# Self-attention heads computed in pairs on small array tiles, and weight rounding in eight pieces

## The chip, the core and the metric

The kernel is one launch on one core of a Trainium2 chip. The core's engines are TensorE (PE), VectorE (DVE), ScalarE (ACT), GpSimd (POOL) and SyncE (SP, which issues the DMAs). The metric is the device time of a launch in microseconds (us).

## The reference

One block of a Perceiver-like model over 256 tokens of width 512: cross-attention to 4096 context rows (16 heads), then self-attention (16 heads of 32 channels), then a feed-forward layer whose weights are rounded to -1, 0 or 1. All of it in float32. The change lies in the second and third parts:

```python
# x: (1, 256, 512)
x = x + _L0_xattn_ref(_layernorm(x), ctx_512, ...)          # cross-attention, untouched
# self-attention, H = 16 heads, Dh = 32
qkv = einsum('bsd,df->bsf', Xn, W_in);  Q, K, V = split(qkv, 3)
Q, K = _rope(Q), _rope(K)
scores = einsum('bhqd,bhkd->bhqk', Q, K) / sqrt(Dh)
probs = softmax(scores, axis=-1)
ctx = einsum('bhqk,bhkd->bhqd', probs, V)
x = X + einsum('bsd,df->bsf', ctx, W_out)
# feed-forward; weight_quant for w1, w2, w3:
scale = 1.0 / clip(mean(abs(w)), EPS)
wq = clip(round(w * scale), -1.0, 1.0) / scale
h = silu(bitlinear(x, w1)) * bitlinear(x, w3);  x = x + bitlinear(h, w2)
```

## The kernel before

The program is written engine by engine. Each engine runs its instructions in the order in which they are written, and semaphores (`wait_ge`, `then_inc`) order them across engines. There are two token tiles t of 128 tokens, and the 16 heads lie in four groups g of four heads a, so that a group fills 128 channels.

Up to about 495 us runs the cross-attention, which the diff doesn't touch. Then come two layer norms, and for each token tile three projections (K, Q, V; `project`, L764). V of tile 1 is done in two halves, the second after the first scores. Queries and keys are copied to SBUF (`natural_copy`), rotated on VectorE (`rotate`, four small instructions with two SBUF inputs, L1356 to L1362), transposed on TensorE, and copied again.

Keys go to `kbd`, a block-diagonal tile: 128 rows (channels of a group) by 16 heads by 256 keys, zero outside the 32 rows of each head (`k_rows`, L367, two copies on VectorE and two on ScalarE for each tile). Values go to `vbd` in the same way (`value_copies`, L1372, four small copies a tile). GpSimd writes the zeros ahead (L533, L535). With the zeros, one full 128-row product gives the scores of one head, for all of its 128 queries.

The attention loop goes by groups. A unit u is a group g and a token tile t, so there are eight units. On TensorE `head_scores(u)` (L802) makes two products of 512 columns. VectorE's `maxima(u)` takes the negated maxima of four heads from PSUM (L1415) and multiplies these 128x4 numbers by the score scale (L1416); ScalarE's `exponentials(u)` (L1091) makes four exponentials with that bias and scale and their sums; `normalise(u)` on VectorE takes a reciprocal (L1406) and multiplies the four heads' probabilities in SBUF (L1408). TensorE transposes the probabilities head by head (`head_transposes`, L814), VectorE and ScalarE copy them out in turns (`probabilities_out`, L1422 and L1099), and `head_product` (L828) multiplies them with `vbd`; the four heads of a group add into one PSUM tile, which VectorE copies out to `cT` (L1454). Two units' scores lie in PSUM at a time (banks 4 to 7). The output projection (L856, L860) and the feed-forward layer follow.

Beside the loop the weights of the feed-forward layer are prepared. ScalarE sums the absolute values in quarters (`abs_sum`, L1047), TensorE and VectorE make a scale of them (`weight_sum`, `weight_total`, `weight_scale`), GpSimd multiplies and rounds each weight in two passes over 128x5632 elements (`weight_magic`, L543, and `weight_round`, L548), and VectorE clips the result (`clip`, L1426). GpSimd's first rounding pass waits for the last projection; each of the magic passes waits for its scale.

Of the kernel before, what the change touches and what calls it, by code (L numbers as in the profile page):

```python
# [5 lines left out]
TOK = 256  # L6
TT = TOK // 128
# [20 lines left out]
def program(nc, x_in, ctxT, kcos, ksin, qcos, qsin, wq, wkcq, wqr, wkr, wkv, wo,  # L28
# [16 lines left out]
    ASCALE = float(DH) ** -0.5  # L45
    ctx = ExitStack()
    with ctx:
# [55 lines left out]
        prob = at("prob", C, [128, 4, HPG, TOK])  # L103
# [66 lines left out]
        anb = small("anb", [128, 8, HPG])  # L170
# [27 lines left out]
        anb_done = sem("anb_done")  # L198
# [5 lines left out]
        bd_zero = sem("bd_zero")  # L204
# [99 lines left out]
        kbd_done = [sem(f"kbd_done{k}") for k in range(2)]  # L304
# [58 lines left out]

        def k_rows(copy, t, a):

            part = slice(a * DH, (a + 1) * DH)
            return copy(kbd[part, a::HPG, t * 128:(t + 1) * 128], bank(t)[part, :].rearrange("p (g k) -> p g k", g=FG))  # L367
# [103 lines left out]
        def _(pool):  # L471
# [60 lines left out]
            pool.wait_ge(av_done, 16 * XH)  # L532
            nc.gpsimd.memset(vbd[:, :, :, :], 0.0).then_inc(bd_zero, 1)  # L533
            pool.wait_ge(xo_done, TT)
            nc.gpsimd.memset(kbd[:, :, :], 0.0).then_inc(bd_zero, 1)  # L535
# [5 lines left out]
            def weight_magic(j, wf):  # L541
                pool.wait_ge(wscale_done, j + 1)
                nc.gpsimd.tensor_scalar(wf[:, :], wf[:, :], wscale[:, j:j + 1], MAGIC, ALU.mult, ALU.add)\  # L543
                    .then_inc(wmagic_done, 1)

            def weight_round(j, wf, wb):
                pool.wait_ge(wmagic_done, j + 1)
                nc.gpsimd.tensor_scalar(wb[:, :], wf[:, :], -MAGIC, 1.0, ALU.add, ALU.mult).then_inc(wround_done, 1)  # L548
# [5 lines left out]
            pool.wait_ge(wround_done, 1)  # L554
# [11 lines left out]
        def _(pe):  # L566
# [213 lines left out]
            for t in range(TT):  # L780
# [5 lines left out]
                if t == 0:  # L786
                    pe.wait_ge(v_copied, HPG)
                    project(1, 2, range(DK // 2))
            def head_scores(u):

                g, t = u // 2, u % 2
                if u == 0:
                    pe.wait_ge(qkn_done, 2 * TT)
                if u == 1:
                    pe.wait_ge(wmean_done, 1)
                if u < 2:
                    pe.wait_ge(qT_done, t + 1)
                wait(pe, aexp_done, 4 * (u - 1))
                for a in range(2):
                    if u == 0:  # L800
                        pe.wait_ge(kbd_done[a], 2 * TT)
                    last = nc.tensor.matmul(bank(4 + u % 2 * 2 + a), qT[:, t, g, :],  # L802
                                            kbd[:, 4 * g + 2 * a:4 * g + 2 * a + 2, :].rearrange("p h k -> p (h k)"),
                                            start=True, stop=True)
                last.then_inc(ascore_done, 1)

            def head_transposes(g, a):

                pe.wait_ge(prob_done, 4 * (2 * g + 1) + a + 1)
                wait(pe, pT_done[a % 2], 2 * g + a // 2)  # L810
                for k in range(TT):
                    for t in range(TT):
                        o = (k * TT + t) * 128
                        last = nc.tensor.transpose(bank(a % 2, o, o + 128),  # L814
                                                   prob[:, (2 * g + t) % 4, a, k * 128:(k + 1) * 128], ident[:, :])
                last.then_inc(apT_done, 1)

            def head_product(g, a):

                if a == 0:  # L820
                    wait(pe, cT_done, g - 1)
                    if g == 1:
                        pe.wait_ge(v_copied, 2 * HPG)
# [756 lines left out]
```

## Time and profile before

| | us |
|---|---|
| median of 3 runs | 617.68 (617.29 to 619.96) |
| the profiled execution, its own time | 613.68 |
| span of its trace | 611.8 |
| mean granted TensorE clock | 0.974 of full |
| TensorE busy, whole span | 549.7 |
| VectorE busy, whole span | 513.5 |
| ScalarE busy, whole span | 369.3 |
| GpSimd busy, whole span | 161.6 |

The span is the time from the first to the last instruction; the launch's own time is 1.9 us longer. Of this execution the stretch from about 512 us to 577 us is the self-attention, and all of the diff lies in it. A row of the trace gives the start, the duration, the engine, the line of the kernel, the operation and the tiles; "x4" means four records in a row, and the bracket at the end names who ended the idle time ahead of it. A float32 product shows as two records.

### The profile page before, as it was taken

Reading aid. Unit: us, or ns where it says so; the run is one execution under the profiler, and the core shown is the slowest. Engines: PE = TensorE matmul, PEld = TensorE weight load, DVE = VectorE, ACT = ScalarE, POOL = GpSimd, SP = SyncE. Lnnn points to the kernel's source line nnn. Section 1 sums busy time; section 2 is a strip of 40 time slices with the busy share of each in tenths; the row PEclk is TensorE's granted clock in tenths of the full one; section 3 lists DMA queues with packets and bytes.
Section 4 is the critical chain, followed back from the end, with each engine's and each line's share of the span. In section 5 each row is a group of like instructions: output and inputs, shape, how many; then the busy total and the mean of one; then the engine's idle time right before and its main releaser. Section 6 shows DMA issues by size and latency. Waiting matters only on the chain.

```text
span 611.8 us, 9932 instructions
## 1 busy us (share of the span) xinstructions
PE 549.7 (90%) x3762; PEld 380.0 (62%) x3762; DVE 513.5 (84%) x782; ACT 369.3 (60%) x435; POOL 161.6 (26%) x148
## 2 busy tenths in 40 slices
PE   6788986838999999999999999999979998688996
PEld 3677774415666666666766676676668854355543
DVE  5478988785989999999999999999968555898786
ACT  3312321583878687877878787878785338654332
POOL 2446678300220221021012202220101243455001
PEclk9799998988999999999999999999999999989999
DMA  9983311799999999999999999999999875000000
GB/s 315 349 245 126 116 54 50 129 361 201 201 195 199 196 196 201 201 210 210 210 209 202 204 197 204 197 203 205 196 193 166 347 276 219 1 0 1 2 0 34
DMA packets 290412, 107.38 MB, mean 176 GB/s; under 512 B 282704, under 2 KB 283728, under 8 KB 288080
## 3 DMA queue, kind: packets, MB, share of 16 engines
q1 hardware_dynamic: 290384, 107.01, 80.5%
q8 instruction: 17, 0.28, 0.2%
q14 instruction: 11, 0.09, 0.0%
HBM read 37.26 MB, written 0.52 MB: 62 GB/s over the span
## 4 chain that ended last, share of the span: by engine, by line
PE 63%; DVE 18%; DMA 6%; issue 5%; ACT 4%; SPq 2%; POOL 1%; DVEq 0%; ACTq 0%; POOLq 0%
PE ps L656 15%; PE ps L658 8%; PE ps L638 8%; PE ps L640 8%; PE ps L639 8%; DMA pT<-split 5%; PE ps L764 3%; PE ps L828 2%; DVE rows L1272 2%; DVE split L1254 2%; DVE qrope L1298 2%; DVE qrot L1304 1%; PE ps L802 1%; DMA keys<-ctxT 1%; PE ps L606 1%
## 5 line engine op out<-in xcount | busy, mean ns | idle before, releaser
L656 PE MATMUL ps<-pT,VH 128*128 128x256 f16 x1024 | 196.2, 273 | 9.3 <-DMA pT<-split 9.2
L658 PE MATMUL ps<-pT,VL 128*128 128x128 f16 x1024 | 182.9, 219 | 0.0
L1272 DVE TENSOR_SCALAR_CACHE_REDUCE rows<-ps,qback 128x1024 f32<-128x1024 f32 x128 | 163.5, 1279 | 23.0 <-PE ps L640 23.0
L1016 ACT ACTIVATE split<-rows,rz 128x2048 f16<-128x2048 f32 x64 | 124.7, 1994 | 75.9 <-DVE rz L1218 73.6
L1254 DVE SCALAR_TENSOR_TENSOR split<-rows,rz,split 128x2048 f16<-128x2048 f32 x64 | 150.2, 2348 | 1.3 <-issue 1.2
L656 PEld LDWEIGHTS ps<-pT,VH 128*128 128x128 f16 x1024 | 100.4, 98 | 49.4 <-issue 10.8
L1002 ACT ACTIVATE rows<-rows,negm 128x2048 f32<-128x2048 f32 x64 | 127.2, 1988 | 2.9 <-DVE negm L1277 2.9
L658 PEld LDWEIGHTS ps<-pT,VL 128*128 128x128 f16 x1024 | 100.5, 98 | 27.6 <-issue 0.3
L521 POOL TENSOR_TENSOR ctx_c<-acc 128x128 f32<-128x128 f32 x32 | 26.0, 814 | 303.1 <-ACT acc L991 303.1
L638 PE MATMUL ps<-KH,qcur 128*128 128x512 f16 x256 | 97.8, 382 | 8.4 <-DVE rows L1272 5.0
L640 PE MATMUL ps<-KH,qcur 128*128 128x512 f16 x256 | 97.8, 382 | 0.0
L639 PE MATMUL ps<-KL,qcur 128*128 128x512 f16 x256 | 97.8, 382 | 0.0
L487 POOL TENSOR_TENSOR qrope<-qrope,qrot 128x768 f32<-128x768 f32 x16 | 35.3, 2205 | 43.2 <-DVE qrot L1304 43.2
L640 PEld LDWEIGHTS ps<-KH,qcur 128*128 128x128 f16 x256 | 25.2, 98 | 30.7 <-issue 0.8
L962 ACT ACTIVATE KH<-keys,kscale 128x512 f16<-128x512 f32 x8 | 5.8, 722 | 55.7 <-DVE keys L1310 46.7
L638 PEld LDWEIGHTS ps<-KH,qcur 128*128 128x128 f16 x256 | 25.2, 99 | 15.3 <-DVE rows L1272 6.7
L719 PE MATMUL ps<-qrope,wqr_sb 128*128 128x256 f32 x96 | 24.5, 392 | 7.0 <-ACT qrT L967 4.0
L639 PEld LDWEIGHTS ps<-KL,qcur 128*128 128x128 f16 x256 | 25.2, 98 | 2.4 <-issue 0.3
L691 PE MATMUL ps<-hT_hi,wq_hi 128*128 128x256 f32 x64 | 20.3, 317 | 6.6 <-ACT qhk L945 5.1
L719 PEld LDWEIGHTS ps<-qrope,wqr_sb 128*128 128x128 f32 x96 | 18.1, 194 | 12.3 <-POOL qrope L487 5.7
L828 PE MATMUL ps<-pT,vbd 128*128 128x256 f32 x64 | 19.2, 438 | 7.0 <-DVE pT L1422 7.0
L703 PE MATMUL ps<-qhk,wkcq_sb 128*128 128x256 f32 x96 | 23.6, 384 | 1.3 <-DVE qrot L1304 1.3
(188 smaller groups left out, 802.2 us busy)
## 6 DMA issues: line engine op xcount, KB each, us to landing
w_sb<-w SPq DMA_DIRECT2D x3, 2816.0 KB, 15.1
wq_sb<-wq SPq DMA_DIRECT2D x4, 1024.0 KB, 8.5
wo_sb<-wo SPq DMA_DIRECT2D x4, 1024.0 KB, 10.8
wkcq_sb<-wkcq SPq DMA_DIRECT2D x4, 768.0 KB, 5.9
keys<-ctxT SPq DMA_DIRECT2D x2, 1024.0 KB, 8.4
stage<-ctxT SPq DMA_DIRECT2D x16, 128.0 KB, 3.2
stage<-kcos SPq DMA_DIRECT2D x8, 256.0 KB, 3.3
stage<-ksin SPq DMA_DIRECT2D x8, 256.0 KB, 3.5
```

What stands on the lines that cost most here:

```text
L487: nc.gpsimd.tensor_tensor(qrope[:, h % 2], qrope[:, h % 2], qrot[:, h % 2], ALU.add).then_inc(qrope_done, 1)
L638: nc.tensor.matmul(o, q[0], KH[:, key], start=True, stop=False)
L639: nc.tensor.matmul(o, q[0], KL[:, key], start=False, stop=False)
L640: last = nc.tensor.matmul(o, q[1], KH[:, key], start=False, stop=True)
L656: nc.tensor.matmul(bank(6 + r % 2, 0, 256), VH[:, 4 * b + k, :], p.rearrange("p x q -> p (x q)"), start=(b == 0 and k == 0), stop=False)
L658: last = nc.tensor.matmul(bank(6 + r % 2, 0, 128), VL[:, 4 * b + k, :], p[:, 0, :], start=False, stop=(b == 7 and k == 3))
L719: last = nc.tensor.matmul(bank(6, 0, TOK), wqr_sb[:, h % 2, h // 2 * QC + c, :], qrope[:, h % 2, c * TOK:(c + 1) * TOK], start=(h % 2 == 0 ...
L828: last = nc.tensor.matmul(bank(2 + g % 2, 0, TOK), vbd[:, k, 4 * g + a, :], pT[:, a, k, :], start=(a == 0 and k == 0), stop=(a == HPG - 1 ...
L1002: nc.scalar.activation(part, part, ACT.Exp, bias=negm[:, k:k + 1], accum_out=zpart[:, k, half:half + 1]).then_inc(exp_done, 1)
L1016: nc.scalar.activation(split[:, split_slot(r, half), :, 0, :], rows[:, k, half * 2048:(half + 1) * 2048].rearrange("p (b k) -> p b k", k=1 ...
L1254: nc.vector.scalar_tensor_tensor(out=split[:, split_slot(r, half), :, 1, :], in0=rows[:, k, half * 2048:(half + 1) * 2048].rearrange("p (b ...
L1272: nc.vector.tensor_scalar(rows[:, k, c * 1024:(c + 1) * 1024], ps[:, score_bank(s) * 512:(score_bank(s) + 2) * 512], qback[:, r // 2:r // ...
```

## The change

- The block-diagonal tiles and the GpSimd passes that zero them are gone. `kT` holds the keys plainly, 128 rows by 4 groups by 256 keys, and `v_sb` the values; each is filled by one copy for each tile.
- A unit v is now a pair of heads of one group, with both token tiles; there are again eight (`UNITS`). The scores of a head come from its 32 rows alone (`tile_position` with a row offset), four products of 256 columns a unit. The products with the values write 32 columns of the array (a column offset), four of 256 columns a unit, and no longer add over the heads.
- The score scale is put into the copy of the queries (`scale=ASCALE` in the copy to `qT`). The 128x4 multiplication of the maxima is gone.
- GpSimd's six weight passes are written as eight pieces of 128x704 each.
- The loop is written in another order on the three engines.

```diff
+    WPIECES = 8
+    UNITS = AH // 2
-        kbd = at("kbd", D + 16 * KB, [128, AH, TOK])
-        vbd = at("vbd", C + 16 * KB, [128, TT, AH, 128])
+        kT = at("kT", D + 16 * KB, [128, FG, TOK])
+        v_sb = at("v_sb", C + 16 * KB, [128, TT, DM])
...
             def weight_magic(j, wf):
                 pool.wait_ge(wscale_done, j + 1)
-                nc.gpsimd.tensor_scalar(wf[:, :], wf[:, :], wscale[:, j:j + 1], MAGIC, ALU.mult, ALU.add)\
-                    .then_inc(wmagic_done, 1)
+                for k in range(WPIECES):
+                    part = slice(k * DK * FF // WPIECES, (k + 1) * DK * FF // WPIECES)
+                    nc.gpsimd.tensor_scalar(wf[:, part], wf[:, part], wscale[:, j:j + 1], MAGIC, ALU.mult, ALU.add)\
+                        .then_inc(wmagic_done, 1)
...
+            def head_scores(v):
+
+                g, first = v // 2, v % 2 * 2
...
+                for t in range(TT):
+                    for x in range(2):
+                        part = slice((first + x) * DH, (first + x + 1) * DH)
+                        last = nc.tensor.matmul(bank(4 + v % 2 * 2 + x, t * TOK, (t + 1) * TOK), qT[part, t, g, :],
+                                                kT[part, g, :], start=True, stop=True, tile_position=((first + x) * DH, 0))
                 last.then_inc(ascore_done, 1)
...
+                for k in range(TT):
+                    for x in range(2):
+                        a = first + x
+                        o = (2 + g % 2) * 512
+                        last = nc.tensor.matmul(ps[a * DH:(a + 1) * DH, o:o + TOK],
+                                                v_sb[:, k, (4 * g + a) * DH:(4 * g + a + 1) * DH], pT[:, a, k, :],
+                                                start=(k == 0), stop=(k == TT - 1), tile_position=(0, a * DH))
...
+            head_scores(0)
+            head_scores(1)
+            for v in range(UNITS):
+                head_transposes(v)
+                if v + 2 < UNITS:
+                    head_scores(v + 2)
...
+                if v >= 1:
+                    head_products(v - 1)
+            head_products(UNITS - 1)
...
+            exponentials(0)
+            for v in range(UNITS):
+                if v + 1 < UNITS:
+                    exponentials(v + 1)
+                probabilities_out(v)
+                if v < 4:
+                    abs_sum(2, v)
...
+            value_copies(1)
+            maxima(0)
+            maxima(1)
+            weight_total(1)
+            for v in range(UNITS):
+                normalise(v)
+                if v + 2 < UNITS:
+                    maxima(v + 2)
...
+                probabilities_out(v)
+                if v == 5:
                     clip(0, w1b)
```

TensorE before, from the last two products of group 0 through the scores and transposes of the units 4 and 5 (`prob` is the probabilities, `pT` their transposes):

```order
L828 MATMUL ps<-pT,vbd 128x256 [waits pT_done1]
L828 MATMUL ps<-pT,vbd 128x256
L802 MATMUL ps<-kbd,qT 128x512 [waits aexp_done]
L802 MATMUL ps<-kbd,qT 128x512
L814 MATMUL ps<-ident,prob 128x128 [waits pT_done0,prob_done]
L814 MATMUL ps<-ident,prob 128x128 x3
L814 MATMUL ps<-ident,prob 128x128 [waits pT_done1,prob_done]
L814 MATMUL ps<-ident,prob 128x128 x3
L802 MATMUL ps<-kbd,qT 128x512 [waits aexp_done]
L802 MATMUL ps<-kbd,qT 128x512
```

TensorE after, one whole unit in the same part of the program:

```order
L813 MATMUL ps<-ident,prob 128x128 [waits pT_done0,prob_done]
L813 MATMUL ps<-ident,prob 128x128 x3
L813 MATMUL ps<-ident,prob 128x128 [waits pT_done1]
L813 MATMUL ps<-ident,prob 128x128 x3
L801 MATMUL ps<-kT,qT 128x256 [waits aexp_done]
L801 MATMUL ps<-kT,qT 128x256 x3
L832 MATMUL ps<-pT,v_sb 32x256 [waits pT_done1,pT_done0]
L832 MATMUL ps<-pT,v_sb 32x256 x3
```

Before, the scores of the group ahead stand in front of the transposes of this one. Now the transposes of a unit stand in front of the scores of the unit two ahead, and the products of the unit behind close the round.

VectorE before, one group of the loop:

```order
L1415 TENSOR_REDUCE anm<-ps 128x4 [waits ascore_done]
L1416 TENSOR_SCALAR anb<-anm 128x4 [waits dve_chain]
L1422 COPY pT<-ps 128x512 [waits apT_done]
L1415 TENSOR_REDUCE anm<-ps 128x4 [waits ascore_done]
L1416 TENSOR_SCALAR anb<-anm 128x4 [waits dve_chain]
L1422 COPY pT<-ps 128x512 [waits apT_done]
L1406 RECIPROCAL arz<-az 128x4 [waits aexp_done]
L1408 TENSOR_SCALAR prob<-prob,arz 128x256 [waits dve_chain]
L1408 TENSOR_SCALAR prob<-prob,arz 128x256 x3
L1406 RECIPROCAL arz<-az 128x4 [waits aexp_done]
L1408 TENSOR_SCALAR prob<-prob,arz 128x256 [waits dve_chain]
L1408 TENSOR_SCALAR prob<-prob,arz 128x256 x3
```

VectorE after, one unit of the loop and the start of the next:

```order
L1391 RECIPROCAL arz<-az 128x4 [waits aexp_done]
L1394 TENSOR_SCALAR prob<-prob,arz 128x256 [waits dve_chain]
L1394 TENSOR_SCALAR prob<-prob,arz 128x256 x3
L1400 TENSOR_REDUCE anm<-ps 128x4 [waits ascore_done]
L1406 COPY pT<-ps 128x512 [waits aav_done,apT_done]
L1391 RECIPROCAL arz<-az 128x4 [waits aexp_done]
L1394 TENSOR_SCALAR prob<-prob,arz 128x256 [waits dve_chain]
```

The L1416 rows are gone. The maxima of a unit now stand right behind the normalisation of the unit two behind it, and ahead of the copy of that unit's transposes.

## Rows read from the trace of the kernel before

**Rows 1.** Busy time by stretch: PE, PEld, DVE, ACT, POOL; clock; DMA.

```profile
533.00:545.00 12.00, 8.97 (x30) 6.35 (x31) 11.86 (x14) 3.51 (x14) 9.84 (x2) 0.73 0.00 0
545.00:557.00 12.00, 12.00 (x54) 8.21 (x53) 9.36 (x30) 9.31 (x28) 0.00 (x0) 1.00 0.01 1
```

**Rows 2.** Chain that ended last, in time: start, us, engine, tile, line.

```profile
514.79 3.23 DVE rot_tmp L1356
...
527.47 4.86 DVE prob L1408 x4
...
535.02 3.92 DVE anb L1416
...
574.85 1.82 PE ps L828 x8
```

**Rows 3.** One line of VectorE over 500 to 612 us: busy, mean ns, idle before.

```profile
L1416 DVE TENSOR_SCALAR anb<-anm 128x4 f32<-128x4 f32 x8 | 14.6, 1822 | 0.3
```

**Rows 4.** Timeline of DVE: a rotation, the loop, and the first clip.

```profile
511.13 0.42 DVE L1356 TENSOR_TENSOR rot_tmp<-qkn,acs 128x256 f32<-128x256 f32 x1 [1.40 <-ACT qkn L1053]
...
546.47 0.18 DVE L1406 RECIPROCAL arz<-az 128x4 f32<-128x4 f32 x1 [0.64 <-ACT prob L1091]
546.68 1.14 DVE L1408 TENSOR_SCALAR prob<-prob,arz 128x256 f32<-128x256 f32 x4
...
548.46 1.22 DVE L1415 TENSOR_REDUCE anm<-ps 128x4 f32<-128x1024 f32 x1 [0.31 <-PE ps L802]
...
549.80 0.69 DVE L1422 COPY pT<-ps 128x512 f32<-128x512 f32 x1
...
571.78 1.61 DVE L1426 TENSOR_SCALAR w1b<-w1b 128x5632 bf16<-128x5632 bf16 x1
```

**Rows 5.** Timeline of POOL in the self-attention: start, us, engine, line, operation.

```profile
533.96 4.96 POOL L543 TENSOR_SCALAR w_sb<-w_sb,wscale 128x5632 f32<-128x5632 f32 x1 [2.55 <-DVE wscale L1384]
```

**Rows 6.** Timeline of PE in the loop.

```profile
532.87 1.97 PE L814 MATMUL ps<-ident,prob 128*128 128x128 f32 x8 [4.30 <-DVE prob L1408]
...
546.54 1.88 PE L802 MATMUL ps<-kbd,qT 128*128 128x512 f32 x4
548.26 1.04 PE L814 MATMUL ps<-ident,prob 128*128 128x128 f32 x8
549.13 1.88 PE L802 MATMUL ps<-kbd,qT 128*128 128x512 f32 x4
```

**Rows 7.** Timeline of ACT, first and fifth exponential of the loop.

```profile
524.50 0.47 ACT L1091 ACTIVATE prob<-ps,anb 128x256 f32<-128x256 f32 x1 [1.40 <-DVE anb L1416]
...
526.31 0.48 ACT L1091 ACTIVATE prob<-ps,anb 128x256 f32<-128x256 f32 x1
```

**Rows 8.** Timeline of DVE in the first stage, where POOL works beside it.

```profile
35.98 0.69 DVE L1310 TENSOR_TENSOR keys<-keys,stage 128x512 f32<-128x512 f32 x1
36.59 1.81 DVE L1223 TENSOR_TENSOR ksum<-kpart 128x1 f32<-128x1 f32 x1
```

**Rows 9.** Timeline of POOL in the same stage.

```profile
36.03 2.35 POOL L487 TENSOR_TENSOR qrope<-qrope,qrot 128x768 f32<-128x768 f32 x1 [5.62 <-DVE qrot L1304]
38.35 1.27 POOL L500 TENSOR_TENSOR keys<-keys,stage 128x512 f32<-128x512 f32 x1
...
71.03 2.31 POOL L487 TENSOR_TENSOR qrope<-qrope,qrot 128x768 f32<-128x768 f32 x1 [3.85 <-DVE qrot L1304]
73.31 1.71 POOL L500 TENSOR_TENSOR keys<-keys,stage 128x512 f32<-128x512 f32 x1
```

**Rows 10.** Timeline of DVE again, a product of keys between two POOL instructions.

```profile
72.46 1.43 DVE L1314 SCALAR_TENSOR_TENSOR KL<-keys,kscale,KH 128x512 f16<-128x512 f32 x1 [0.79 <-ACT KH L962]
```

**Rows 11.** Busy time by half microsecond, columns as in Rows 1.

```profile
518.00:518.50 0.50, 0.00 (x0) 0.00 (x0) 0.47 (x4) 0.50 (x1) 0.00 (x0) 1.00 0.00 0
...
533.00:533.50 0.50, 0.50 (x3) 0.50 (x4) 0.50 (x3) 0.00 (x0) 0.00 (x0) 0.50 0.00 0
...
536.50:537.00 0.50, 0.50 (x2) 0.00 (x0) 0.50 (x1) 0.00 (x0) 0.50 (x1) 1.00 0.00 0
```

More of the change, by code:

```diff
@@ L303, in program @@
         zsum_done = sem("zsum_done")
-        kbd_done = [sem(f"kbd_done{k}") for k in range(2)]
+        kT_done = sem("kT_done")
         ctx_in = [sem(f"ctx_in{k}") for k in range(2)]
@@ L795, in head_scores @@
                     pe.wait_ge(wmean_done, 1)
[L796 to L804, printed above, removed]
@@ L805, in head_scores @@
-                last.then_inc(ascore_done, 1)
[L807 to L816, printed above, removed]
@@ new lines, in head_scores, with head_transposes @@
+                last.then_inc(ascore_done, 1)
+            def head_transposes(v):
+                pe.wait_ge(prob_done, 4 * (v + 1))
+                for x in range(2):
+                    wait(pe, pT_done[x], v)
+                    for k in range(TT):
+                        for t in range(TT):
+                            o = (k * TT + t) * 128
+                            last = nc.tensor.transpose(bank(x, o, o + 128), prob[:, v % 4, x, t, k * 128:(k + 1) * 128],
+                                                       ident[:, :])
+                    last.then_inc(apT_done, 1)
@@ L821, in head_product, with head_products @@
+            def head_products(v):
+                g, first = v // 2, v % 2 * 2
+                if first == 0:
                     wait(pe, cT_done, g - 1)
-                    if g == 1:
-                        pe.wait_ge(v_copied, 2 * HPG)
+                    if g == 0:
+                        pe.wait_ge(v_copied, 2)
                     if g % 2 == 0:
                         pe.wait_ge(wmean_done, g // 2 + 2)
-                pe.wait_ge(pT_done[a % 2], 2 * g + a // 2 + 1)
+                for x in range(2):
+                    pe.wait_ge(pT_done[x], v + 1)
@@ L1084, in _ @@
             abs_sum(1, 3)
-            def exponentials(u, first=0, end=HPG):
-                act.wait_ge(anb_done, u + 1)
-                if u >= 4:
-                    act.wait_ge(apT_done, 4 * (u // 2 - 1))
-                for a in range(first, end):
-                    nc.scalar.activation(prob[:, u % 4, a, :], bank(4 + u % 2 * 2 + a // 2, a % 2 * TOK, (a % 2 + 1) * TOK),
-                                         ACT.Exp, bias=anb[:, u, a:a + 1], scale=ASCALE,
-                                         accum_out=az[:, u, a:a + 1]).then_inc(aexp_done, 1)
@@ L1418, in probabilities_out, with normalise @@
-            def probabilities_out(g, a):
-                dve.wait_ge(apT_done, 4 * g + a + 1)
-                wait(dve, aav_done, 4 * (g - 1) + a + 1)
-                nc.vector.tensor_copy(pT[:, a].rearrange("p k t -> p (k t)"), bank(0)).then_inc(pT_done[0], 1)
+            def normalise(v):
+                dve.wait_ge(aexp_done, 4 * (v + 1))
+                link(nc.vector.reciprocal(arz[:, v, :], az[:, v, :]))
+                for k in range(4):
+                    part = prob[:, v % 4, k // 2, k % 2, :]
+                    nc.vector.tensor_scalar(part, part, arz[:, v, k:k + 1], None, ALU.mult).then_inc(prob_done, 1)
@@ new lines, in maxima, with probabilities_out @@
+            def maxima(v):
+                dve.wait_ge(ascore_done, v + 1)
+                b = 4 + v % 2 * 2
+                src = ps[:, b * 512:(b + 2) * 512].rearrange("p (a k) -> p a k", a=4)
+                nc.vector.tensor_reduce(anm[:, v, :], src, AX.X, ALU.max, negate=True).then_inc(anm_done, 1)
+            def probabilities_out(v):
+                dve.wait_ge(apT_done, 2 * v + 1)
+                wait(dve, aav_done, v - 1)
+                nc.vector.tensor_copy(pT[:, v % 2 * 2].rearrange("p k t -> p (k t)"), bank(0)).then_inc(pT_done[0], 1)
@@ L1455, in _ @@
+            context_copy(FG - 1)
+            clip(1, w3b)
             clip(2, w2b)
```

159 lines of the change are left out of this document (48 added, 111 removed).

## Prediction, made before the changed kernel was run

> **What bounds the kernel now.** I read four views. First the table by stretch [rows 1]: between 545 and 557 us, where GpSimd rests, TensorE is busy for 12.00 of 12.00 us at full clock; in the stretch before, where GpSimd works for 9.84 us, TensorE falls to 8.97 of 12, its clock to 0.73, and VectorE is busy for 11.86. Second the chain of waits in time [rows 2]: the last product of the loop ends at 574.85 + 1.82 = 576.67 us, and the chain runs through three kinds of long VectorE rows, a rotation of 3.23 us, four normalisations of 4.86 us together, a 128x4 multiplication of 3.92 us. Third the line of those 128x4 multiplications [rows 3]: eight of them take 14.6 us. Fourth the timelines: four normalisations alone take 1.14 us [rows 4], and the 3.92 us one of the chain begins at 535.02 and ends at 538.94, as GpSimd's pass ends (533.96 + 4.96 = 538.92, [rows 5]). So VectorE instructions of this kind, from SBUF to SBUF, stand still until GpSimd's instruction is over. Reductions and copies out of PSUM do not.
>
> The stalls add up to about 20 us: 14.6 less eight times 0.17 gives 13.2, the normalisations 4.86 less 1.14 give 3.7, and the rotation 3.23 less the 0.42 us of its like [rows 4] gives 2.8. What is left is bound by TensorE.
>
> The Trainium skill, "SBUF — State Buffer", section "SBUF: two separate sides", says that VectorE and GpSimd share a pair of ports as an exclusive lock, held for a whole instruction, with the loser fully blocked. The stalls above agree. The page does not say who comes next when both wait.
>
> **What goes and what takes its place, with GpSimd and the clock left out.** The new loop is one chain per unit. On VectorE a unit's normalisation stands ahead of the maxima of the unit two ahead; TensorE has transposes ahead of the scores that these maxima wait for. Nothing of this overlaps. The terms:
> - normalisation 0.21 + 1.14 = 1.35 [rows 4], and 0.05 to reach TensorE;
> - transposes of two heads 549.13 - 548.26 = 0.87 [rows 6];
> - scores. Before, two products of 512 columns take 548.26 - 546.54 = 1.72 [rows 6]. Four of 256 columns are as many columns. No row shows array tiles: if both row tiles run side by side it is half, 0.86; if not, 1.72 and whatever a change of tile shape costs. Below 0.86 nothing can go, since two tiles are used. Each float32 product is two records, and records of one head must follow each other, so only the second of one head and the first of the next overlap; I take 1.3;
> - 0.20 from TensorE to VectorE (548.26 to 548.46), maxima 1.22, copy of the transposes 0.60 of its 0.69 [rows 4, 6].
>
> Together 5.6 us a unit (5.15 to 6.0). Before, a unit where GpSimd rests costs 1.72 + 0.87 + 1.82 = 4.4, TensorE's own work [rows 2, 6]. So the pairs relieve TensorE, which then idles, and put a latency chain in its place.
>
> The start: the rotation begins at 514.8, takes 1.2 alone (the 0.42 of its first instruction [rows 4], and 0.8 for the three behind it), and about 0.3 + 3 x 0.65 more by GpSimd's pieces (below); with 0.44 of transposes and 1.73 of the second half of V it puts the first scores at 520.4, against 521.05. The copies to kT (2 in place of 4) and v_sb are hidden behind that half of V; were they not, they would cost 0.7. Then 1.3 + 0.2 + 1.22 and four exponentials at (526.31 - 524.50)/4 = 0.45 each with 0.2 to hand over [rows 7]: the first normalisation at 525.2. Six units of 5.6 reach 558.8. VectorE also has in this chain one clip of 1.6 [rows 4], two copies to cT of 0.34 and two weight scales of 0.33, together 3.0: 561.8. The last two units lack scores and maxima: 2.6 to the last normalisation, then 1.35 + 0.9 + 0.2 + 0.6 + 0.1 and a product of 1.3 (0.87 to 1.82): **568.9**, 7.8 less than 576.67. The ScalarE work in a unit (1.8 of exponentials, 0.5 of copy, 1.5 of sums in the first four) is under 5.6 and hidden; if the unit were shorter than 3.9 it would bind. The removed zeroing passes ran while GpSimd had nothing else due: nothing. The clips of w3 and w2, now 3.2 us behind the last cT copy, lie beside 4.3 us of output projection: nothing, a slack of 1.1.
>
> **GpSimd in pieces.** A piece is 4.96/8 = 0.62 us [rows 5]; I allow 0.05 between pieces. Forty of the 48 lie in the loop. What counts is who goes next when both engines want the pair. The first stage shows both sides [rows 8, 9]. At 35.98 VectorE multiplies keys, GpSimd's L487 starts at 36.03 and waits; VectorE's next, L1223, one element wide, stands directly behind (36.59) and still takes 1.81 us, to 38.40, as L487 ends at 38.38. So a waiting GpSimd goes ahead of a queued VectorE instruction. In the other direction, L500 at 73.31, queued right behind L487, takes 1.71 us against 1.27 at 38.35 [rows 9], since VectorE's L1314, waiting since 72.46 [rows 10], goes first. The two take turns. A long pass made VectorE wait once; now the four multiplications of a unit each wait for a piece: 0.3 for the first and 0.65 for the other three, 2.25 a unit. Forty pieces with VectorE's turns between them take 27 + 5 = 32 us of a loop of some 45, so about five of eight units: 5 x 2.25 + 0.3 for the clip = **11.5**. Bounds: 1.8 (one wait of 0.3 for each) and 18 (all eight). This gives 580.4, 3.7 later than before.
>
> **The clock.** Before, TensorE idled for 4.30 us to 532.87 [rows 6]; at 533.0 the granted clock is 0.50, its lower level of 1.2 GHz, and at 536.5 again 1.00, after TensorE had worked through [rows 11]. Eight transposes took 1.97 there in place of 1.04. A shorter pause at 518 left it at 1.00 [rows 11]. In a unit with pieces TensorE now idles from the end of a product to the next transposes: 0.2 + 1.22 + 0.6 + 1.35 + 2.25 - 1.3 = 4.3 us, the length that made it fall. Transposes and scores, 2.2 us of the chain, then double, for as long as the stretch above (533.0 to under 536.5, some 3.5 us) lasted: 1.75 lost each time. I take three in the five units: **5.3** (0 to 8.8); units without pieces idle for 2.0 and cost nothing. Sum: 568.9 + 11.5 + 5.3 = 585.7, **9.0 later**. Everything behind the loop (the output projection and the feed-forward) keeps its order and length. The profiled execution took 613.68, so 622.7 by it; the median of the runs is 4.0 higher, and on that I forecast 617.68 + 9.0 = 626.7.
>
> **Rivals.**
> - *Turns, but the clock holds*: 3.7 later, 621.4. For: small matrices keep TensorE working more often than in one block. Against: the idle time of 4.3. Chance 0.20.
> - *VectorE keeps the pair over its four multiplications*, since they come back to back and overlap. Then 1.8 stands for 11.5, idle times shrink, two falls of the clock at most: 568.9 + 1.8 + 3.5 = 574.2, 2.5 earlier, 615.2, and 611.7 with no fall. It decides from the point where a unit waits less than about 0.5 us, one piece. Against: L1223, which also stood back to back. Chance 0.18, two thirds of it faster.
> - *The array tiles don't overlap, and each change of shape costs*: scores at 1.72 and 0.2 (as long as TensorE takes to hand a result over, the nearest row) at two changes in a unit's chain: 0.82 x 6 + 1 = 6 more, 632.7. Chance 0.14.
> - The forecast: 0.48.
>
> The Trainium skill has two rules on this. "TensorE: Matmul & The Clock Gate", "Part 3: Packing small matmuls — row/col tiling", has several tiles take one product's time and some 4 ns for each tile more; by it the scores are 0.87, and the end 3 us earlier, 623.7. "TensorEngine Tiling (Array Packing)", "Key Properties", speaks against the change: a change of tiling mode drains TensorE, and there are three in each unit; that is the third rival. No row here shows either.
>
> **How the numbers follow.** About 0.5% (3.1 us) is what this kernel's measurement tells from no change: 614.6 to 620.8. Faster: two thirds of the second rival, 0.12. Same: the rest of it and half of the first, 0.16. Slower: 0.72. The range goes from 614 (second rival with one fall) to 634 (third rival with a little more): about one in ten on each side.
>
> **What would show it.** Right: L1394's total is far over 32 x 0.28 = 9 us, with many rows near 0.9 us in the stretches where GpSimd works, while reductions stay at 1.2; the granted clock is 0.50 in several stretches of the loop; normalisation to normalisation takes 5.6 in a quiet unit. Wrong: L1394 rows wait once a unit (second rival), four score products take 0.86 or over 1.9 us at full clock, or GpSimd's pieces take well over 0.67 with nobody waiting. The end of the loop, 576.67 before, is the one number to compare.

## The result, and the profile after

The changed kernel takes 626.52 us (median of 4 runs, 624.9 to 628.32) against 617.48 for the kernel before: ratio 1.0139, 95% interval 1.0094 to 1.0183. That is slower, by 9.0 us or 1.4%, clear of the noise but a small change. The profiled execution took 625.16, its span is 623.4. The loop that the diff rewrites runs from the first scores to the first product of the output projection, from 520.89 to 587.98 us: 67.1 us, against 55.5 before (521.05 to 576.51). What follows it takes as long as before (623.4 - 588.0 = 35.4, before 611.8 - 576.5 = 35.3). So the loss lies in the loop.

Busy time by stretch of the changed kernel (us, PE, PEld, DVE, ACT, POOL, granted clock, DMA), as in [rows 1] and [rows 11]:

```profile
522.00:523.50 1.50, 0.04 (x4) 0.00 (x0) 1.43 (x2) 0.92 (x3) 1.50 (x3) 1.00 0.00 0
...
525.00:526.50 1.50, 0.00 (x0) 0.00 (x0) 1.17 (x3) 1.50 (x9) 1.50 (x3) 0.50 0.00 0
...
553.50:555.00 1.50, 1.50 (x9) 1.17 (x9) 0.00 (x0) 0.10 (x1) 0.00 (x0) 0.50 0.00 0
...
583.50:585.00 1.50, 1.50 (x8) 0.76 (x5) 0.10 (x1) 0.00 (x0) 0.00 (x0) 0.50 0.00 0
...
586.50:588.00 1.50, 1.50 (x17) 0.60 (x12) 0.00 (x0) 1.48 (x2) 0.00 (x0) 1.00 0.00 0
```

TensorE pauses from about 522.0 us, its clock falls during this first pause (at about 524.7 us), and it stays at 0.50, the lower level of 1.2 GHz, until about 586.1 us, 2 us before the end of the loop. TensorE's rows show both the chain and the clock; the bracket is the pause ahead of the row:

```profile
520.89 1.16 PE L801 MATMUL ps<-kT,qT 32*128 32x256 f32 x16
527.78 1.97 PE L813 MATMUL ps<-ident,prob 128*128 128x128 f32 x8 [5.74 <-DVE prob L1394]
...
545.74 1.97 PE L813 MATMUL ps<-ident,prob 128*128 128x128 f32 x8 [2.88 <-DVE prob L1394]
547.63 2.08 PE L801 MATMUL ps<-kT,qT 32*128 32x256 f32 x8
549.64 1.92 PE L832 MATMUL ps<-pT,v_sb 128*32 128x256 f32 x8
552.90 1.97 PE L813 MATMUL ps<-ident,prob 128*128 128x128 f32 x8 [1.33 <-DVE prob L1394]
...
586.15 1.91 PE L832 MATMUL ps<-pT,v_sb 128*32 128x256 f32 x16
```

A unit's transposes take 1.97 us where the same eight records took 1.04 at full clock before [rows 6]. From 545.74 to 552.90 TensorE works for 5.8 of 7.2 us and the clock does not rise; it does behind 580.49, from where TensorE works almost without a pause. That work is transposes and products on small tiles (`128*32`), so the small tiles of the products don't by themselves keep the clock down. The first pause is 5.7 us long, the others 1.3 to 5.0.

VectorE's normalisations (groups of four, and below them one group and GpSimd's pieces beside it one by one):

```profile
534.00 2.97 DVE L1394 TENSOR_SCALAR prob<-prob,arz 128x256 f32<-128x256 f32 x4
...
551.70 1.14 DVE L1394 TENSOR_SCALAR prob<-prob,arz 128x256 f32<-128x256 f32 x4
```

```profile
534.00 0.39 DVE L1394 TENSOR_SCALAR prob<-prob,arz 128x256 f32<-128x256 f32 x1
534.32 0.94 DVE L1394 TENSOR_SCALAR prob<-prob,arz 128x256 f32<-128x256 f32 x1
535.17 0.94 DVE L1394 TENSOR_SCALAR prob<-prob,arz 128x256 f32<-128x256 f32 x1
536.04 0.94 DVE L1394 TENSOR_SCALAR prob<-prob,arz 128x256 f32<-128x256 f32 x1
```

```profile
533.39 0.86 POOL L537 TENSOR_SCALAR w_sb<-w_sb,wscale 128x704 f32<-128x704 f32 x1 [6.33 <-DVE wscale L1370]
534.23 0.88 POOL L537 TENSOR_SCALAR w_sb<-w_sb,wscale 128x704 f32<-128x704 f32 x1
535.09 0.88 POOL L537 TENSOR_SCALAR w_sb<-w_sb,wscale 128x704 f32<-128x704 f32 x1
535.95 0.88 POOL L537 TENSOR_SCALAR w_sb<-w_sb,wscale 128x704 f32<-128x704 f32 x1
```

Each multiplication ends 0.15 us behind the end of a piece, one for one: the two engines take turns, with a period of 0.86 us. With nobody waiting the same pieces come every 0.83 us, so a turn costs GpSimd hardly anything and VectorE almost all. Alone the four take 1.14 us. Five of the eight groups meet pieces (2.22, 2.97, 2.69, 2.95, 2.69 us), 7.8 us above five times 1.14. The clip in the loop adds 0.25 (1.86 for 1.61).

### The profile page after: what moved, and what is told of

Same layout as the page of the kernel before. It is cut to its first block, busy times and chain, and to the rows that moved or that the text cites. A ratio compares the mean times of both kernels' runs of the same rounds, so it can differ in the third digit from the quotient of the medians.

```text
span 623.4 us, 10004 instructions
## 1 busy us (share of the span) xinstructions
PE 550.0 (88%) x3791; PEld 378.4 (61%) x3794; DVE 499.7 (80%) x766; ACT 367.3 (59%) x431; POOL 165.7 (27%) x188
## 4 chain that ended last, share of the span: by engine, by line
PE 59%; DVE 21%; DMA 7%; issue 5%; ACT 3%; SPq 3%; POOL 1%; DVEq 0%; ACTq 0%; POOLq 0%
PE ps L653 14%; PE ps L655 7%; PE ps L637 6%; PE ps L635 6%; PE ps L636 6%; DMA pT<-split 6%; DVE rows L1263 3%; PE ps L761 3%; PE ps L813 3%; DVE prob L1394 3%; PE ps L801 2%; DVE split L1245 2%; DVE qrope L1289 2%; DVE qrot L1295 2%; SPq L445 1%
## 5 line engine op out<-in xcount | busy, mean ns | idle before, releaser
L1015 ACT ACTIVATE split<-rows,rz 128x2048 f16<-128x2048 f32 x64 | 124.8, 1996 | 76.3 <-DVE rz L1209 74.0
L813 PE MATMUL ps<-ident,prob 128*128 128x128 f32 x64 | 15.7, 427 | 24.3 <-DVE prob L1394 24.3
L537 POOL TENSOR_SCALAR w_sb<-w_sb,wscale 128x704 f32<-128x704 f32 x24 | 20.7, 883 | 38.9 <-DVE wscale L1370 38.9
L813 PEld LDWEIGHTS ps<-ident,prob 128*128 128x128 f32 x64 | 12.5, 223 | 30.0 <-DVE prob L1394 30.0
L1400 DVE TENSOR_REDUCE anm<-ps 128x4 f32<-128x1024 f32 x8 | 9.7, 1224 | 24.8 <-PE ps L801 24.8
```

Source lines behind the costliest of these rows:

```text
L813: last = nc.tensor.transpose(bank(x, o, o + 128), prob[:, v % 4, x, t, k * 128:(k + 1) * 128], ident[:, :])
L1015: nc.scalar.activation(split[:, split_slot(r, half), :, 0, :], rows[:, k, half * 2048:(half + 1) * 2048].rearrange("p (b k) -> p b k", k=1 ...
```

## The experiments

Kernels a1 to a7 start from the changed kernel, b1 to b5 from the one before. The loop is measured as above in the profiled execution, since it begins up to 5 us earlier or later from one profiled execution to the next (519.4 to 524.8 us). The profiled execution of the kernel before was 3.8 us shorter than its median of 617.48, so loops are best compared among the others: against 55.5 they come out some 1 to 7 us worse than the ratios say.

| kernel | median us | ratio to before (95%) | loop us |
|---|---|---|---|
| before | | | 55.5 |
| changed | 626.52 | 1.0139 (1.0094 to 1.0183) | 67.1 |
| a1, passes whole | 636.58 | 1.0278 (1.023 to 1.0326) | 76.3 |
| a2, fillers | 618.42 | 0.9993 (0.9961 to 1.0025) | 59.1 |
| a3, exponentials in PSUM | 626.16 | 1.0165 (1.012 to 1.021) | 66.4 |
| a4, a3 and fillers | 611.03 | 0.9888 (0.9825 to 0.995) | 50.6 |
| a5, score order | 626.17 (one run) | | 66.7 |
| a6, a3 and clips moved | 619.65 | 1.003 (0.9999 to 1.0062) | 60.2 |
| a7, a4 and clips moved | 608.28 | 0.9818 (0.9776 to 0.9861) | 48.8 |
| b1, scale folded | 615.01 | 0.9939 (0.9914 to 0.9964) | 54.8 |
| b2, pieces | 611.26 | 0.9884 (0.9837 to 0.9931) | 53.6 |
| b3, b1, b2 and PSUM | 607.56 | 0.9844 (0.98 to 0.9888) | 48.1 |
| b4, b3 and clip moved | 604.55 | 0.9756 (0.9711 to 0.9802) | 47.0 |
| b5, b4 and fillers | 602.78 | 0.9727 (0.9656 to 0.9798) | 43.6 |

**a1: the pieces undone.** 

```diff
-    WPIECES = 8
+    WPIECES = 1
```

> The changed kernel with its GpSimd passes whole again (one piece of 128x5632 in place of eight). Theory (the two engines take turns, one instruction each): a long pass costs the pairs more than pieces do, since the normalisation that meets the two passes of w3, one behind the other, waits for the rest of the first (about 4.4 us) and, behind its first multiplication, for the whole of the second (4.9 us), and the same again for w2; with 1.5 more in the rotation that is about 20 us of waits in place of the 9.3 measured with pieces, so the loop ends some 10 to 12 us later than 588.05 and the time is near 637. Rival (pieces are what costs, four waits a unit in place of one for a pass): about 4 us earlier, 622.

Measured 636.58. VectorE and GpSimd around the two passes of w3:

```profile
535.68 9.89 DVE L1394 TENSOR_SCALAR prob<-prob,arz 128x256 f32<-128x256 f32 x4
```

The first three of them one by one:

```profile
535.68 4.49 DVE L1394 TENSOR_SCALAR prob<-prob,arz 128x256 f32<-128x256 f32 x1
540.09 0.33 DVE L1394 TENSOR_SCALAR prob<-prob,arz 128x256 f32<-128x256 f32 x1
540.35 4.96 DVE L1394 TENSOR_SCALAR prob<-prob,arz 128x256 f32<-128x256 f32 x1
```

```profile
535.07 4.96 POOL L537 TENSOR_SCALAR w_sb<-w_sb,wscale 128x5632 f32<-128x5632 f32 x1 [6.59 <-DVE wscale L1370]
540.18 4.98 POOL L544 TENSOR_SCALAR w3b<-w_sb 128x5632 bf16<-128x5632 f32 x1 [0.16 <-POOL w_sb L537]
```

The first multiplication waits for the rest of the first pass. The second begins before GpSimd asks again (its second pass starts at 540.18, 0.16 us behind the first) and takes 0.33. The third waits for the whole of the second pass: 9.89 us in place of 1.14. At w2, where the passes stand 0.08 us apart, only one goes between them (4.47 us, then 5.05), 9.96 together. One or two multiplications between two passes, not four: once GpSimd asks, it comes next. This is turn-taking, and it decides against the rival "VectorE keeps the pair over its four multiplications". Within the changed kernel the pieces are worth 9 to 10 us (loops and medians); they are not what made it slow.

**b2: the pieces alone, in the kernel before.** `weight_round` is cut in the same way, and the clips wait for eight times as many rounds.

```diff
                 pool.wait_ge(wscale_done, j + 1)
-                nc.gpsimd.tensor_scalar(wf[:, :], wf[:, :], wscale[:, j:j + 1], MAGIC, ALU.mult, ALU.add)\
-                    .then_inc(wmagic_done, 1)
+                for k in range(WPIECES):
+                    part = slice(k * DK * FF // WPIECES, (k + 1) * DK * FF // WPIECES)
+                    nc.gpsimd.tensor_scalar(wf[:, part], wf[:, part], wscale[:, j:j + 1], MAGIC, ALU.mult, ALU.add)\
+                        .then_inc(wmagic_done, 1)
```

> The kernel before, with its GpSimd passes in eight pieces and nothing else changed. Theory (turns): each of the four long 128x4 multiplications (3.92, 3.30, 3.45, 3.23 us) falls to under 0.8, 11 us less; the first normalisation falls from 4.86 to about 3; but the normalisations of units 1 to 3 and 4 to 6, which met no pass before, now meet pieces and take 1.8 more each. Sum about 6 us less (2 to 9), 611.5, and fewer falls of the clock. Rival (pieces add more waits than they remove): 2 us more, 620.

Measured 611.26, as the theory has it. VectorE, two of the L1416 multiplications (now L1422) and the two normalisations behind them:

```profile
534.56 0.65 DVE L1422 TENSOR_SCALAR anb<-anm 128x4 f32<-128x4 f32 x1
...
537.17 0.52 DVE L1422 TENSOR_SCALAR anb<-anm 128x4 f32<-128x4 f32 x1
...
538.59 3.28 DVE L1414 TENSOR_SCALAR prob<-prob,arz 128x256 f32<-128x256 f32 x4
...
541.99 2.98 DVE L1414 TENSOR_SCALAR prob<-prob,arz 128x256 f32<-128x256 f32 x4
```

The single multiplications fall from 3.92 and 3.30 to 0.65 and 0.52 us; the normalisations, which met no pass before, take 1.8 to 2.1 more. A piece helps the instruction that waits once and burdens the four that stand in a row.

**b1: the scale alone, in the kernel before.**

```diff
-                nc.scalar.activation(qT[:, t, :, :].rearrange("p g t -> p (g t)"), bank(2), ACT.Copy)\
+                nc.scalar.activation(qT[:, t, :, :].rearrange("p g t -> p (g t)"), bank(2), ACT.Copy, scale=ASCALE)\
...
-                nc.vector.tensor_scalar(anb[:, u, :], anm[:, u, :], ASCALE, None, ALU.mult).then_inc(anb_done, 1)
```

> The kernel before with only the score scale moved into the copy of the queries, so that the eight 128x4 multiplications (14.6 us, 13.2 of them waiting for GpSimd) are gone. Theory (turns: the next VectorE instruction that needs the pair takes over the wait): the normalisations behind them now wait for the rest of the same pass and the one after it; of the 13.2 us some 3 are won (1.5 for each pair of passes), 614.5. Rival (the wait goes with the instruction): 13 us less, 604.5.

Measured 615.01. VectorE's normalisation now takes over the wait. It begins when GpSimd's second pass over w3 has just begun (GpSimd's row below), and waits for all of it:

```profile
541.36 5.57 DVE L1408 TENSOR_SCALAR prob<-prob,arz 128x256 f32<-128x256 f32 x4
```

```profile
541.12 4.88 POOL L548 TENSOR_SCALAR w3b<-w_sb 128x5632 bf16<-128x5632 f32 x1 [0.16 <-POOL w_sb L543]
```

Removing the waiting instruction removes 13.2 us of waits from its line and 3.6 us from the kernel.

**a2: TensorE's pauses filled.** Products of `identb` that nobody reads:

```diff
+            pe.wait_ge(v_copied, 2)
+            fill(44, 3)
             for v in range(UNITS):
                 head_transposes(v)
...
                 if v >= 1:
                     head_products(v - 1)
+                fill(FILLS[v], 3 if v == 0 else 2 + (v - 1) // 2 % 2)
```

> The changed kernel with small bfloat16 products that nobody reads put into TensorE's pauses of the loop (44 ahead of the first transposes, then 36, 26, 26, 16, 16, 26, 26 behind the products of each unit, about 0.11 us each at full clock), to see what the low clock costs. Theory (the clock is at 0.50 because of the pauses, and this costs 0.98 us for each unit's transposes, 1.0 for its scores): granted clock 1.00 through the loop, transposes 0.99 and scores 1.03 a unit, 14.9 us less, of which some 3 go back since more units meet pieces of GpSimd: loop end 573 to 577, time 611 to 615. Rival (the clock was low for another reason, or the fillers stand in the way of the chain): 626 or more.

Measured 618.42, above the interval that I gave. The granted clock is 1.00 from 514 to 571 us and the terms are as expected, but the fillers were badly dosed. TensorE:

```profile
549.66 1.03 PE L814 MATMUL ps<-ident,prob 128*128 128x128 f32 x8
550.63 1.13 PE L802 MATMUL ps<-kT,qT 32*128 32x256 f32 x8
...
572.05 1.80 PE L814 MATMUL ps<-ident,prob 128*128 128x128 f32 x8 [3.16 <-DVE prob L1404]
...
575.64 3.07 PE L841 MATMUL ps<-identb 128*128 128x256 bf16 x26
578.54 1.03 PE L814 MATMUL ps<-ident,prob 128*128 128x128 f32 x8
```

At 549.66 the transposes have no pause ahead of them: they stood behind fillers, 0.7 us after VectorE was done (547.84 + 1.14). At the end VectorE was done at 573.85 + 1.14 = 574.99 and the transposes began at 578.54, 3.5 us late. And a pause of 3.16 us was left where the clip stands, behind which the clock fell once more. So this run shows that the clock is worth at least 8 us, not what it is worth.

**a3: the wait on GpSimd taken away.** The exponentials are written back to their PSUM bank and the normalisation reads it there.

```diff
-                        nc.scalar.activation(prob[:, v % 4, x, t, :], bank(4 + v % 2 * 2 + x, t * TOK, (t + 1) * TOK),
+                        b = bank(4 + v % 2 * 2 + x, t * TOK, (t + 1) * TOK)
+                        nc.scalar.activation(b, b,
...
-                    nc.vector.tensor_scalar(part, part, arz[:, v, k:k + 1], None, ALU.mult).then_inc(prob_done, 1)
+                    src = bank(4 + v % 2 * 2 + k // 2, k % 2 * TOK, (k % 2 + 1) * TOK)
+                    nc.vector.tensor_scalar(prob[:, v % 4, k // 2, k % 2, :], src, arz[:, v, k:k + 1], None,
+                                            ALU.mult).then_inc(prob_done, 1)
```

> The changed kernel with the exponentials written back into their PSUM bank, so that the normalisation reads PSUM and writes SBUF; order, pieces and products are the same. Theory (an instruction that reads PSUM doesn't take turns with GpSimd): the 7.8 us of waits in the five units with pieces go, each multiplication takes some 0.35 in place of 0.28 alone, 2 us more in all; GpSimd's pieces shrink to 0.62. Loop 6 us shorter. The clock falls as before in the first pause (4.8 us) and stays at 0.50, since the pauses of 1.3 to 1.7 us between units didn't raise it in the changed kernel: 620.5. Rival (the waits have another cause, the read of PSUM costs as much): 626 or more. Second rival (shorter pauses let the clock rise): 12 less on top, 608.

Measured 626.16: by the total my theory fell. VectorE:

```profile
534.12 1.66 DVE L1397 TENSOR_SCALAR prob<-ps,arz 128x256 f32<-128x256 f32 x4
...
572.97 6.00 DVE L1419 TENSOR_SCALAR w1b<-w1b 128x5632 bf16<-128x5632 bf16 x1
```

GpSimd at the same time:

```profile
571.49 6.00 POOL L544 TENSOR_SCALAR w2b<-w_sb 128x704 bf16<-128x704 f32 x8
```

All eight normalisations take 1.66 us, with pieces beside them or not: the wait is gone there. But the clip of w1, which took 1.86 in the changed kernel, now takes 6.00. It waits for six pieces in a row, until GpSimd has none left, and TensorE pauses for 8.10 us behind it. Turn-taking failed this time.

**a6: was it the clip?** The clips of w1 and w3 moved into VectorE's pauses where GpSimd rests:

```diff
                 normalise(v)
+                if v in (3, 4):
+                    clip(v - 3, (w1b, w3b)[v - 3])
                 if v + 2 < UNITS:
                     maxima(v + 2)
...
-                if v == 5:
-                    clip(0, w1b)
```

> The run with the exponentials in PSUM, no fillers, and the VectorE clips of w1 and w3 (128x5632, SBUF to SBUF) moved out of the stretches where GpSimd works, into VectorE's pauses of 4.08 us behind the normalisations of the fourth and fifth unit; in a3_psum the first of them took 6.00 us, of which 4.4 waiting for six pieces of GpSimd one after the other, and TensorE paused for 8.10 us. Theory (this one clip took back what the normalisations had won): 6 us less than 626.16, 620. Rival (the clock, which stays at 0.50, or something else took it back): 624 or more.

Measured 619.65: it was. The clock stays at 0.50 here too; its pause behind the sixth unit is 2.18 us in place of 8.10.

**a4 and a7: both repairs together.** a4 is a3 with fillers, a7 moves the clips as in a6 as well. Against a2:

```diff
-    FILLS = (36, 26, 26, 16, 16, 26, 26, 0)
+    FILLS = (28, 16, 16, 16, 20, 36, 6, 0)
...
-            fill(44, 3)
+            fill(40, 3)
```

and in a7 18 in place of 36.

> The same with filling products in TensorE's pauses (40 ahead of the first transposes, then 28, 16, 16, 16, 20, 36, 6), fewer than in a2 where that run's fillers stood in the way (0.7 us at the fourth unit, 3.5 at the last). Theory (two costs that add: turns and clock): a unit of 0.98 transposes, 1.03 scores, 1.25 maxima, 0.6 copy and 1.6 normalisation, 5.5 us; six of them, the clip and the short last two: the loop lasts some 47 to 49 us from its first scores against 67.2 in the changed kernel and 55.6 before: 606 to 610. Rival (a floor that neither explains, such as ScalarE's exponentials and sums, 3.8 a unit, or the fillers themselves): over 612.

> a4_psum_fill with the same two clips moved, and 18 fillers fewer at the sixth unit, where the clip stood. Theory: the clip of 1.84 us in the chain goes into a pause of 2.26 at no cost: 1.8 to 2.2 less than a4_psum_fill (611.03), 609. Rival (the pairs' chain has other slack there, or the clip delays the maxima): as a4_psum_fill.

Measured 611.03 and 608.28. a7 came as expected; a4 lies between the theory's range and the rival's, and its loop of 50.6 us is 1.6 above the 49 that I gave. TensorE in a4, one unit:

```profile
541.61 1.09 PE L814 MATMUL ps<-ident,prob 128*128 128x128 f32 x8 [0.83 <-DVE prob L1407]
542.63 1.13 PE L802 MATMUL ps<-kT,qT 32*128 32x256 f32 x8
543.69 1.06 PE L833 MATMUL ps<-pT,v_sb 128*32 128x256 f32 x8
544.68 1.95 PE L841 MATMUL ps<-identb 128*128 128x256 bf16 x16
547.47 1.09 PE L814 MATMUL ps<-ident,prob 128*128 128x128 f32 x8 [0.83 <-DVE prob L1407]
```

The granted clock is 1.00 over the whole loop (521 to 586 us; 0.53 in the changed kernel), and a unit takes 5.86 us, of which the read of PSUM is 0.5. In the two lists of groups the transposes fall from 15.7 to 8.7 us and the scores from 13.6 to 8.0: 12.6 us of clock, all of it in the chain. a6 against a7, which differ in the fillers alone, says nearly the same: 11.4 us.

**a5: do the array tiles overlap by their order?**

```diff
-                for t in range(TT):
-                    for x in range(2):
+                for x in range(2):
+                    for t in range(TT):
                         part = slice((first + x) * DH, (first + x + 1) * DH)
```

> The changed kernel with the four score products of a unit in another order: both of one head, then both of the other, so that neighbours use the same 32 rows of the array. Theory (products on different rows overlap, on the same rows they follow each other): the scores of a unit take 2.03 us at clock 0.50 in the changed kernel; now only the two in the middle overlap and they take 2.7 to 3.0, six units 4 to 6 us more in the loop. Rival (the array overlaps nothing, or reorders by itself): 2.03 as before.

The scores of a unit take 2.08 us, to the hundredth as in the changed kernel. Between neighbours the order doesn't matter. That the tiles overlap is shown elsewhere, by TensorE's rows of the changed kernel and of a2, both at full clock:

```profile
520.89 1.16 PE L801 MATMUL ps<-kT,qT 32*128 32x256 f32 x16
```

```profile
530.14 1.13 PE L802 MATMUL ps<-kT,qT 32*128 32x256 f32 x8
```

The first two units together use all four row tiles, and their 16 records take as long as the 8 of one unit. A unit alone takes 1.06 us from its start to the next row's, where half of the full array's 1.72 [rows 6] is 0.86: the overlap is nearly full, 0.20 short.

**b3 and b4: the same repairs without pairs.** b3 is the kernel before with the folded scale, the exponentials in PSUM and the pieces; the scores wait for the normalisation of the unit that held their bank. b4 moves the clip of w1:

```diff
-                wait(pe, aexp_done, 4 * (u - 1))
+                wait(pe, prob_done, 4 * (u - 1))
...
-                if g == FG:
-                    clip(0, w1b)
+                if g == 2:
+                    clip(0, w1b)
                 if g in (0, 2):
                     weight_scale(g // 2 + 1, bank(2, TOK, TOK + 1))
```

> The kernel before with full-array products and its own order, the score scale in the copy of the queries, the exponentials written back to PSUM, and GpSimd's passes in pieces: all of the waits on the pair of the loop are gone without pairs of heads. Theory (without waits the old loop is bound by TensorE at 4.4 us a unit, less than the 5.5 of the pairs' chain): loop of 40 to 46 us from its first scores against 55.6, 603 to 608, so faster than the pairs with the same repairs. Rival (the scores now wait for the normalisation, which frees their bank, and the chain binds here too): 609 to 612, no better than pieces alone (611.26).

> b3_fold_psum_pieces with VectorE's clip of w1 moved from behind the last rounds, where it took 4.87 us among GpSimd's pieces, to a place ahead of w2's scale, where GpSimd rests. Theory: 3.3 us of waits go, of them 2.5 to 3.3 in TensorE's pauses (2.45 and part of 1.10), and the clip delays the next maxima by up to 1.6, which TensorE's backlog of 5 us hides: 2.5 less than 607.56, 605. Rival (the output projection or the products bind there anyway): 607.5.

Measured 607.56 and 604.55. The medians are within what was expected, but b3's loop of 48.1 us is longer than the 40 to 46 that I gave. In b3 the clip again waits for pieces to the last:

```profile
565.53 4.87 DVE L1434 TENSOR_SCALAR w1b<-w1b 128x5632 bf16<-128x5632 bf16 x1
```

Almost without waits, the full-array loop is shorter than that of the pairs with the same repairs and fillers besides (b4 47.0 against a7 48.8 us), although the scores and products of a unit take TensorE 1.72 and 1.82 us there [rows 2, 6] in place of 1.06 and 0.99. Here the loop that keeps TensorE at work beats the one that relieves it.

**b5: the clock in the old loop.** Fillers in two pauses of b4:

```diff
+            fill(10, 5)
             for g in range(FG + 1):
+                if g == 1:
+                    fill(20, 0)
                 if g < FG:
                     head_scores(2 * g)
```

> b4_clip with filling products in the two pauses of TensorE behind which its clock stood at 0.50: 10 in the 1.46 us ahead of the first scores and 20 in the 2.64 us ahead of the scores of the second group (each 0.11 us). Theory (the low clock costs the full-array loop too): the first two units' scores take 3.5 in place of 5.37 us, the scores and transposes behind the second pause 2.8 in place of 4.5, of which the chain through maxima and exponentials gives about 3 us to the end: 601.5. Rival (both lie beside VectorE's and ScalarE's work and are hidden): 604.5, as b4_clip.

Measured 602.78, the fastest of all; 1.8 us less than b4, where I expected 3. TensorE's first scores in b4, and in b5:

```profile
522.85 5.37 PE L808 MATMUL ps<-kbd,qT 128*128 128x512 f32 x8 [1.46 <-DVE kbd L368]
```

```profile
522.60 3.67 PE L808 MATMUL ps<-kbd,qT 128*128 128x512 f32 x8 [0.35 <-DVE kbd L368]
```

The loops of the two profiled executions differ by 3.4 us, the medians by less; the two ratios' intervals overlap, so the size of this step stays uncertain.

## Why the prediction was right, point by point

The forecast was 626.7 and the median is 626.52, but three of its terms were off and cancelled. The sum was made for the end of the loop, 585.7; it came at 588.0.

- **What bounds the kernel before, and the turns: right.** VectorE's multiplications and two-input instructions with their operands in SBUF wait for GpSimd, what reads PSUM doesn't (a3, b3), and behind a GpSimd instruction one of VectorE's goes, two where GpSimd asked again 0.16 us late (a1, b2). "From SBUF to SBUF" was too wide, though: the reciprocals of the sums (128x4, SBUF to SBUF) take 0.17 us in the middle of a pass too (b1 at 529.31 us, the pass from 528.57 to 533.45), and the reduction `wtot` 0.15 (a1). By the Trainium skill, "SBUF — State Buffer", section "SBUF: two separate sides", the lock is held for a whole instruction; the 4.49 and 4.96 us of a1 agree.
- **The chain without GpSimd and clock: right, 1.8 too long.** a7's loop of 48.8 us, less the 4.2 that reading PSUM costs (8 times 1.66 - 1.14), plus a clip of 1.6 and begun at 520.9, ends at 567.1, by this estimate; I had 568.9. The quiet unit was forecast at 5.6. In the changed kernel it took 559.25 - 551.70 = 7.55, so that sign of being right did not come; at full clock in a2 it is 554.15 - 547.84 = 6.31 less 0.7 behind fillers, so 5.6. Two misses cancel in it: its scores took 1.06 and not 1.3, its transposes 1.0 and not 0.87. My reason for 1.3, that only neighbours in the order overlap, was wrong (a5).
- **Array tiles: between full overlap (0.86) and my 1.3.** They overlap, and something is added each time. At full clock transposes take 1.02 (0.97 in a2, where no pause stands ahead of them), scores 1.06, products 0.99 from start to start, where as many columns take 0.87, 0.86 and 0.91 in the kernel before (548.26 to 549.13, half of 1.72, half of 1.82, [rows 2, 6]): 0.08 to 0.20 each, 0.4 a unit. The third rival had this size about right (0.2) and the missing overlap wrong. That it is the price of a change of shape is argued and not shown: no run has small tiles without a change. The Trainium skill, "TensorEngine Tiling (Array Packing)", section "Key Properties", says that a change of tiling mode drains the array; these rows would fit. The Trainium skill, "TensorE: Matmul & The Clock Gate", "Part 3: Packing small matmuls — row/col tiling", has four tiles in hardly more than one product's time; that four tiles take 1.16 us where two take 1.13 agrees, but the 0.87 that I worked out by it for the scores was 1.06.
- **Turns: mechanism right, 3.4 too high.** 11.5 forecast, 8.1 measured (7.8 and the clip's 0.25). Five units met pieces, as forecast, but a unit paid 1.1 to 1.8 and not 2.25: the first multiplication mostly met a gap (0.39), the others waited for 0.86 - 0.27 = 0.59 or less, and in the first unit the pieces ended half-way. A piece itself was under-sized: I took 0.62, an eighth of a pass; the 48 pieces take 40.4 us together where six passes took 29.5. With nobody waiting one takes 0.83, "well over 0.67": that sign of being wrong came, and it was outweighed by the waits being fewer.
- **The clock: mis-sized, the step that failed.** I forecast 5.3 us, at most 8.8, from three falls of 3.5 us each in the units with pieces, and "units without pieces idle for 2.0 and cost nothing". There was one fall, in the first pause, and no return for 60 us. It cost 12.6 us in transposes and scores (all in all 11.4 between a6 and a7), and 0.9 in the seventh unit's products. I had priced the falls by how long the clock stayed low in the kernel before, where TensorE worked without a pause behind each fall [rows 11]; in a chain with a pause in every unit it has no such stretch. I also never priced the first pause of 5 us, which the chain itself contained.
- **Sum.** 567.1 + 8.1 + 13.5 = 588.7, against 588.0. Of the nearness of 626.7 and 626.52 part is luck: the terms' errors are -1.8, -3.4 and +8.2, and the profiled execution lay 2.5 above its forecast of 622.7 while its median lies only 1.4 above it, where I had taken the 4.0 of the kernel before.
- **Rivals.** "Turns, but the clock holds" was wrong on the clock; its price of 621.4 is 3 above what a2, with all its faults, takes. The second is excluded by a1, the third half right.
- **Behind the loop: right**, 35.4 us against 35.3.

## What to carry to other kernels

Before a loop on TensorE is made leaner, ask which engine its pauses will wait for: here less work on the array only lengthened its pauses, the pauses halved its clock, and the halved clock lay in the chain. Here the clock came back only where TensorE worked without pauses (behind 580.49 us), so one fall cost the rest of the loop and not one lapse for each pause; fillers are a cheap test and, if they are counted so that none stands ahead of work that is due, a cheap repair.

A wait on GpSimd does not go with the instruction that shows it. It moves to the next VectorE instruction of its kind (b1). In these runs it went where the operand comes from PSUM (a3, b3) or the instruction stands where GpSimd rests (a6).

## What the runs showed that I had not expected

- **Turn-taking is not assured.** VectorE's four-fold multiplications always got their turn among pieces. A clip, 128x5632 in bfloat16 and 1.61 us alone, met pieces in nine kernels. In four (the changed one, a2, a4, a5; 1.81 to 2.17 us) it went ahead of the next piece. In four it waited for all that were left: six in a3 (6.00), four whole ones in b3 (4.87), one and the rest of another in b4 and b5 (w3's clip, 2.46 and 2.42). In b2 none was queued behind the one that it met. In b3 it began 0.38 us into a piece, in the changed kernel, where it took 1.86, 0.40 us into one. All four that lost have their exponentials in PSUM, but so has a4, which won. Why a clip loses its turn is open.
- **A pause doesn't fix the clock's fate.** Pauses of 1.84 and 1.45 us ahead of the first scores left the clock at 1.00 in b1 (those scores took 3.67 us), while 0.45 and 1.46 at the same place in b4 were followed by 0.50 (5.37 us).
- **GpSimd in pieces costs GpSimd.** 0.83 us (128x704, float32 to float32) and 0.74 (to bfloat16) from start to start with nobody waiting, against 0.62 and 0.61 for an eighth of a whole pass.
